# The last normalization of a sorted expert layer: computed on VectorE or on GpSimd

## The chip, the cores and the metric

The kernel runs on one core of a Trainium2 chip as a single program. The metric is the device time of one execution in microseconds (us), lower is better. A core has five engines with a queue of instructions each, which run side by side and are ordered only by semaphores: TensorE (PE in the profile: matmuls, PEld: its weight loads), VectorE (DVE), ScalarE (ACT), GpSimd (POOL) and SyncE (SP, which starts DMAs here). Each queue runs in its written order, so an instruction that waits holds everything behind it on its engine.

## The reference, cut to what matters

The reference has four sub-layers on 4096 tokens of 128 channels: a softmax attention, an attention with a mixture of experts behind it, a state-space layer, and a mixture of eight experts of which the last one selected computes a token. Each is followed by a layer norm. The change touches the very end, the layer norm behind the last mixture:

```python
def _layernorm(x, axis=-1, eps=1e-05):
    m = jnp.mean(x, axis=axis, keepdims=True)
    v = jnp.var(x, axis=axis, keepdims=True)
    return (x - m) / jnp.sqrt(v + eps)
...
    for i in range(E):
        wi = w_flat[:, i:i + 1]
        h = jax.nn.relu(jnp.einsum('nd,hd->nh', x_flat * wi, w1[i]) + b1[i])
        y = jnp.einsum('nh,dh->nd', h, w2[i]) + b2[i]
        out = jnp.where(wi > 0, y, out)
...
x = _layernorm(x + _L1_ffn_ref(x, ...), axis=-1)
```

## The kernel before, in words

Stage by stage the kernel runs the four sub-layers, with a barrier between stages. The last stage, `sorted_experts_stage` (from L1985), is the one that is changed. Before it the tokens have been sorted by expert into 40 tiles (`SORT_TILES`) of 128 tokens each, in DRAM; a record holds a token's 128 channels, its gate and the row of the output to which it belongs. The stage then works tile by tile, and every engine has a part:

- SP loads the records in 10 chunks of four tiles (`PER` is 4).
- DVE multiplies a chunk by its gates (`weigh`, L2146), PE transposes it (`turn`, L2055), ACT copies it to SBUF (`copy`, L2100).
- DVE copies the expert's first weights, 516 numbers a partition, into a ring of three (`fetch`, L2138).
- PE runs four matmuls up (L2067), ACT applies bias and ReLU to three of the four results (L2123), DVE to the fourth (`activate`, L2156), and PE runs four matmuls down (L2080), which form the tile's result in one of two places in PSUM.
- POOL adds the second bias to the residual (`add_bias`, L2217) into a ring of four (`RING` is 4).
- DVE adds that to the matmul's result (`add`, L2166), which frees the place in PSUM: `down(t)` waits for the sum of tile t-2.
- DVE takes the statistics (L2171, L2177), ACT turns the variance into 1/sqrt(variance + eps) by Ln and Exp (`invert`, L2104 and L2109), and DVE normalizes (`normalize`, L2183): one instruction, 128x128, that subtracts the mean and multiplies by the inverse, both of them one number a partition.
- POOL starts an indirect DMA that scatters the tile's 128 rows to their places in the output (`scatter`, L2222).

The order on each engine is written out by hand. DVE's loop for tile t is activate(t), fetch(t+2), statistics(t-1), for one t in four a weigh, aggregate(t-1), add(t), normalize(t-2). POOL's is add_bias(t+3), scatter(t). Rings tie them together: `add(t)` and `aggregate(t)` wait for the normalization of tile t-4, `add_bias(t)` for the sum of tile t-4, and `normalize(t)` for the landing of the scatter of tile t-4. POOL reads the tile's expert number into a register ahead of each add_bias (L2212).

Of the kernel before, what the change touches and what calls it, by code (L numbers as in the profile page):

```python
# [9 lines left out]
ALU = mybir.AluOpType  # L10
# [1779 lines left out]
SORT_TILES = (N + E * (TILE - 1)) // TILE + 1  # L1790
# [194 lines left out]
def sorted_experts_stage(core, scratch, tile_expert, w1, w2, b2, ident, out):  # L1985
# [7 lines left out]
    nc = core.nc  # L1993
# [4 lines left out]
    RING = 4  # L1998
    SLOTS = 3
    with ExitStack() as st:  # L2000
# [7 lines left out]
        total = core.sb("f_total", [TILE, RING, D], F32, st)  # L2008
        stats = core.sb("f_stats", [TILE, RING, 6], F32, st)
        mean_var = core.sb("f_mean_var", [TILE, RING, 2], F32, st)  # L2010
        log_var = core.sb("f_log_var", [TILE, RING], F32, st)
        inverse = core.sb("f_inverse", [TILE, RING], F32, st)
        normed = core.sb("f_normed", [TILE, RING, D], F32, st)
# [23 lines left out]
        with nc.Block() as block:  # L2037
# [93 lines left out]
            @block.vector  # L2131
            def _(dve):
                def fetch(t):
                    e = dve.value_load(tile_expert[0:1, t:t + 1], min_val=0, max_val=E - 1)  # L2134
                    if t >= SLOTS:
                        dve.wait_ge(low_done, t - SLOTS + 1)
                        dve.wait_ge(high_done, t - SLOTS + 1)
                    nc.vector.tensor_scalar(weights[:, t % SLOTS, :], w1[:, ds(e, 1), :].rearrange("p a n -> p (a n)"), 1.0,  # L2138
                                            None, ALU.mult).then_inc(fetched, 1)

                def weigh(c):
                    dve.wait_ge(loaded[c], 16)
                    if c >= 2:
                        dve.wait_ge(turned_done, c - 1)
                    of = slice(c * PER, (c + 1) * PER)
                    nc.vector.tensor_tensor(weighted[:, c % 2, :, :], records[:, of, 0:D],  # L2146
                                            records[:, of, D:D + 1].broadcast_to([TILE, PER, D]),
                                            ALU.mult).then_inc(weighted_done, 1)

                def activate(t):  # L2150
                    dve.wait_ge(up_done, t + 1)
                    if t >= 2:
                        dve.wait_ge(down_done, t - 1)
                    for f in range(BY_ACT, HIDDEN):
                        at = f - BY_ACT
                        last = nc.vector.tensor_scalar(high[:, t % 2, at, :], high_ps[:, t % 2, at * TILE:(at + 1) * TILE],  # L2156
                                                       weights[:, t % SLOTS, HIDDEN * D + f:HIDDEN * D + f + 1],
                                                       0.0, ALU.add, ALU.max)
                    last.then_inc(high_done, 1)

                def add(t):
                    dve.wait_ge(biased_done, t + 1)
                    if t >= RING:
                        dve.wait_ge(normed_done, t - RING + 1)
                    dve.wait_ge(down_done, t + 1)
                    nc.vector.tensor_tensor(total[:, t % RING, :], out_ps[:, t % 2, 0:D], biased[:, t % RING, :],  # L2166
                                            ALU.add).then_inc(total_done, 1)

                def spread_of(t):
                    dve.wait_ge(total_done, t + 1)  # L2170
                    nc.vector.bn_stats(stats[:, t % RING, :], total[:, t % RING, :]).then_inc(stats_done, 1)  # L2171

                def aggregate(t):
                    dve.wait_ge(stats_done, t + 1)
                    if t >= RING:
                        dve.wait_ge(normed_done, t - RING + 1)
                    nc.vector.bn_aggr(mean_var[:, t % RING, :], stats[:, t % RING, :]).then_inc(mean_var_done, 1)  # L2177

                def normalize(t):
                    dve.wait_ge(inverse_done, t + 1)  # L2180
                    if t >= RING:
                        dve.wait_ge(scattered[t % RING], 16 * (t // RING))
                    nc.vector.tensor_scalar(normed[:, t % RING, :], total[:, t % RING, :], mean_var[:, t % RING, 0:1],  # L2183
                                            inverse[:, t % RING:t % RING + 1], ALU.subtract, ALU.mult).then_inc(normed_done, 1)

                nc.vector.memset(eps[:, :], EPS).then_inc(eps_set, 1)
                fetch(0)
                fetch(1)
                weigh(0)
                weigh(1)  # L2190
                for t in range(SORT_TILES):
                    activate(t)
                    if t + 2 < SORT_TILES:
                        fetch(t + 2)
                    if t:
                        spread_of(t - 1)
                    if t % PER == 1 and t // PER + 2 < CHUNKS:
                        weigh(t // PER + 2)
                    if t:
                        aggregate(t - 1)  # L2200
                    add(t)
                    if t >= 2:
                        normalize(t - 2)
                spread_of(SORT_TILES - 1)
                normalize(SORT_TILES - 2)
                aggregate(SORT_TILES - 1)
                normalize(SORT_TILES - 1)

            @block.gpsimd
            def _(pool):  # L2210
                def add_bias(t):
                    e = pool.value_load(tile_expert[0:1, t:t + 1], min_val=0, max_val=E - 1)  # L2212
                    if t % PER == 0:
                        pool.wait_ge(loaded[t // PER], 16)
                    if t >= RING:
                        pool.wait_ge(total_done, t - RING + 1)
                    nc.gpsimd.tensor_tensor(biased[:, t % RING, :], records[:, t, 0:D],  # L2217
                                            b2[:, ds(e, 1), :].rearrange("p a n -> p (a n)"), ALU.add).then_inc(biased_done, 1)

                def scatter(t):  # L2220
                    pool.wait_ge(normed_done, t + 1)
                    nc.gpsimd.indirect_dma_start(out, bass.IndirectOffsetOnAxis(ap=records[:, t, D + 1:D + 2].bitcast(U32), axis=0),  # L2222
                                                 normed[:, t % RING, :], None).then_inc(scattered[t % RING], 16)

                for t in range(RING - 1):
                    add_bias(t)
                for t in range(SORT_TILES):
                    if t + RING - 1 < SORT_TILES:
                        add_bias(t + RING - 1)
                    scatter(t)  # L2230
                for r in range(RING):
                    pool.wait_ge(scattered[r], 16 * (SORT_TILES // RING))

# [208 lines left out]
```

## Time and profile before

| | us |
|---|---|
| median of three runs | 1810.93 (1808.12 to 1813.86) |
| the profiled execution | 1810.93 |
| its span, from the first to the last instruction | 1808.9 |
| the last stage, from SP's first load of records (1704.12) to the end of the span | 104.8 |

The profiled execution is 2.0 us longer than its span. Its granted TensorE clock is 0.921 of full speed on average over the span. Busy time is the time in which an engine runs an instruction; register, branch, semaphore and DMA-issuing instructions are not counted, but the indirect DMA on POOL is, for the time in which POOL prepares it. An arrow in a row (`<-DVE f_normed L2183`) names what ended the idle time ahead of the instruction. Tiles of the last stage have names that begin with f_.

### The profile page before, as it was taken

How to read it: one execution, taken by the hardware profiler on the slowest of the kernel's cores; microseconds unless marked ns; L12 is line 12 of the kernel's file. 1: busy time of each engine (PE TensorE's matmuls, PEld its weight loads, DVE VectorE, ACT ScalarE, POOL GpSimd, SP SyncE). 2: the span in 40 equal slices, each digit the busy share in tenths (PEclk: the TensorE clock that was granted, in tenths of full speed). 3: DMA queues.
4: the chain of work that ended last, by engine and by line, in shares of the span. 5: the costliest groups of instructions: out<-in, count | busy, mean ns of one | idle time of the engine just before them, and what ended most of it. 6: DMA issues, size and time to landing. Idle time of an engine off the chain costs nothing. (4 is left out here: it accounts for less than half of the span.)

```text
span 1808.9 us, 38945 instructions
## 1 busy us (share of the span) xinstructions
PE 1559.3 (86%) x13976; PEld 841.8 (47%) x13976; DVE 1310.8 (72%) x1816; ACT 1262.9 (70%) x2366; POOL 525.5 (29%) x742
## 2 busy tenths in 40 slices
PE   5999999999979999999999999949999653662297
PEld 4555555555534444434344443337777221222286
DVE  3777777777679999999999999334554459655176
ACT  2777777777637998898899998838887577131165
POOL 0222222222144101100100111029999033213566
PEclk8999999999978999999999999879999866785599
DMA  2021110000013110010011000034554000022300
GB/s 79 22 87 52 52 22 18 17 18 17 17 31 110 27 26 4 13 31 10 5 31 33 16 25 4 1 49 96 85 84 67 15 0 0 0 111 77 96 30 32
DMA packets 40102, 68.39 MB, mean 38 GB/s; under 512 B 9192, under 2 KB 20208, under 8 KB 39472
## 3 DMA queue, kind: packets, MB, share of 16 engines
q1 hardware_dynamic: 34608, 59.87, 14.1%
q0 software_dynamic: 5376, 6.96, 1.4%
q8 instruction: 72, 1.18, 0.3%
q14 instruction: 46, 0.38, 0.1%
HBM read 32.56 MB, written 7.77 MB: 22 GB/s over the span
## 5 line engine op out<-in xcount | busy, mean ns | idle before, releaser
L903 ACT ACTIVATE m_probs<-m_ring 128x512 f32<-128x512 f32 x1024 | 543.3, 598 | 83.4 <-PE m_ring L825 67.5
L972 DVE TENSOR_REDUCE m_half_max<-m_pairs 128x2 f32<-128x1024 f32 x512 | 587.7, 1212 | 12.6 <-PE m_pairs L808 12.1
L387 DVE TENSOR_REDUCE a_neg_max<-a_scores 128x1 f32<-128x1024 f32 x257 | 310.4, 1214 | 91.0 <-PE a_scores L314 91.0
L375 ACT ACTIVATE a_probs<-a_scores,a_neg_max 128x1024 f32<-128x1024 f32 x256 | 285.1, 1114 | 123.5 <-DVE a_neg_max L387 123.5
L840 PE MATMUL m_acc<-m_probs,m_v_aug 128*32 128x256 f32 (+1 forms) x4032 | 330.6, 401 | 0.0
L825 PE MATMUL m_ring<-m_q_max,m_k 32*128 32x512 f32 x1024 | 319.6, 503 | 3.8 <-DVE m_q_max L986 2.9
L808 PE MATMUL m_pairs<-m_k,m_q 32*128 32x512 f32 x1024 | 264.0, 513 | 13.1 <-DVE m_half_max L972 9.6
L314 PE MATMUL a_scores<-a_q,a_k_own 64*128 64x512 f32 x516 | 260.1, 620 | 6.5 <-ACT a_probs L375 5.6
L314 PE MATMUL a_scores<-a_q,a_k_other 64*128 64x512 f32 x516 | 258.4, 620 | 0.7 <-ACT a_probs L375 0.2
L825 PEld LDWEIGHTS m_ring<-m_q_max,m_k 32*128 32x128 f32 x1024 | 146.7, 184 | 219.2 <-ACT m_probs L903 115.0
L422 POOL TENSOR_TENSOR a_scaled<-values,a_inv 128x128 f32<-128x128 f32 x256 | 102.1, 399 | 389.0 <-DVE a_inv L405 258.0
L1403 POOL TENSOR_TENSOR e_g_parts<-e_gated,e_g_parts 128x512 fp32r<-128x512 f32 x128 | 165.1, 1319 | 32.9 <-ACT e_g_parts L1343 31.9
L1374 DVE TENSOR_TENSOR e_gated<-e_up,e_gates 128x512 f32<-128x512 f32 x128 | 87.5, 689 | 97.2 <-ACT e_up L1336 82.6
L324 PE MATMUL a_mixed<-a_probs,a_scaled 128*32 128x128 f32 x4128 | 139.3, 276 | 0.0
L840 PEld LDWEIGHTS m_acc<-m_probs,m_v_aug 128*32 128x32 f32 x4032 | 80.4, 109 | 125.4 <-ACT m_probs L903 79.0
L324 PEld LDWEIGHTS a_mixed<-a_probs,a_scaled 128*32 128x32 f32 x4128 | 104.9, 109 | 56.2 <-issue 30.3
L314 PEld LDWEIGHTS a_scores<-a_q,a_k_other 64*128 64x128 f32 x516 | 86.0, 187 | 65.3 <-issue 32.8
L808 PEld LDWEIGHTS m_pairs<-m_k,m_q 32*128 32x128 f32 x1024 | 97.5, 187 | 28.1 <-DVE m_half_max L972 23.2
L1336 ACT ACTIVATE e_up<-e_up,e_b 128x512 f32<-128x512 f32 x128 | 84.4, 659 | 33.7 <-PE e_up L1298 33.5
L314 PEld LDWEIGHTS a_scores<-a_q,a_k_own 64*128 64x128 f32 x516 | 86.0, 187 | 33.3 <-issue 24.4
L1054 POOL CAST m_max_cols<-m_row_max 128x16 fp32r<-128x16 f32 x32 | 6.8, 211 | 281.3 <-DVE m_row_max L978 280.8
L1309 PE MATMUL e_acc<-e_g_parts,m_q 128*128 128x512 f32 x256 | 80.2, 395 | 2.9 <-POOL e_g_parts L1403 2.9
(256 smaller groups left out, 2086.6 us busy)
## 6 DMA issues: line engine op xcount, KB each, us to landing
e_gates<-sorted_results SPq DMA_DIRECT2D x64, 256.0 KB, 8.0
a_k_other<-a_k_own SPq DMA_DIRECT2D x66, 128.0 KB
m_k<-m_k_init SPq DMA_DIRECT2D x8, 512.0 KB, 3.9
m_q<-xT SPq DMA_DIRECT2D x8, 512.0 KB, 4.4
sorted_tokens<-q_blank SPq DMA_DIRECT2D x5, 544.0 KB, 6.4
f_records<-sorted_tokens SPq DMA_DIRECT2D x10, 272.0 KB, 5.2
e_w<-e_w_dram SPq DMA_DIRECT2D x1, 2064.0 KB, 7.8
xT<-x_t_dram SPq DMA_DIRECT2D x1, 2048.0 KB, 7.7
```

Of the source, the lines that this page charges most:

```text
L314: last = nc.tensor.matmul(scores[:, slot(i), h * BANK:(h + 1) * BANK], keys[rows, p, g // 2, :], q[rows, p, :, :].rearrange("p g t -> p (g ...
L324: last = nc.tensor.matmul(mixed[32 * j:32 * j + 32, :], scaled[:, g, j, 32 * e:32 * e + 32], probs[:, g, (2 * j + e) * TILE:(2 * j + e + 1 ...
L375: nc.scalar.activation(probs[:, g, :], scores[:, slot(h * G + g), :], ACT.Exp, bias=neg_max[:, g:g + 1], accum_out=total[:, g:g + 1]).then ...
L387: nc.vector.tensor_reduce(neg_max[:, i % G:i % G + 1], scores[:, slot(i), :], AX, ALU.max, negate=True).then_inc(max_done, 1)
L422: nc.gpsimd.tensor_tensor(scaled[:, g, :, :].rearrange("p j (e c) -> p j e c", c=48)[:, :, :, 0:16], values[:, ds(b * G, G), 16 * g:16 * g ...
L808: last = nc.tensor.matmul(pairs[:, pair % 2, m, :], q[batch % 2][rows, g, at:at + TILE], k[batch % 2][rows, g, a * BANK:(a + 1) * BANK], s ...
L825: nc.tensor.matmul(o, k[batch % 2][rows, n % GROUPS, u * TILE:(u + 1) * TILE], q_max[rows, number % 2, :], start=True, stop=True).then_inc ...
L840: last = nc.tensor.matmul(acc[32 * j:32 * j + 32, of], v_aug[:, g, u, j, :], probs[:, u % SLOTS, j, of], start=(g == 0 and u == 0), stop=( ...
L903: nc.scalar.activation(probs[:, u % SLOTS, head, :], ring[:, bank, :], ACT.Exp, scale=0.5).then_inc(ring_taken, 1)
L972: nc.vector.tensor_reduce(half_max[:, pair // PAIRS % 2, at:at + 2], pairs[:, pair % 2, :, :], AX, ALU.max).then_inc(pair_taken, 1)
L1374: nc.vector.tensor_tensor(gated[:, n % R, :], up[:, n % R, :], gates[:, c % 2, e, :], ALU.mult).then_inc(gated_done, 1)
L1403: nc.gpsimd.tensor_tensor(g_parts[:, 1, n % R, :], gated[:, n % R, :], g_parts[:, 0, n % R, :].bitcast(F32), ALU.subtract).then_inc(lo_don ...
```

## The change

The instruction that normalizes a tile moves from DVE to POOL, just ahead of the scatter that reads it, and POOL waits for its own result before it issues the scatter. POOL prepares the biased residual two tiles ahead of the scatter's tile instead of three. The two loops:

```diff
@@ DVE
-                def normalize(t):
-                    dve.wait_ge(inverse_done, t + 1)
-                    if t >= RING:
-                        dve.wait_ge(scattered[t % RING], 16 * (t // RING))
-                    nc.vector.tensor_scalar(normed[:, t % RING, :], total[:, t % RING, :], mean_var[:, t % RING, 0:1],
-                                            inverse[:, t % RING:t % RING + 1], ALU.subtract, ALU.mult).then_inc(normed_done, 1)
...
                     add(t)
-                    if t >= 2:
-                        normalize(t - 2)
                 spread_of(SORT_TILES - 1)
-                normalize(SORT_TILES - 2)
                 aggregate(SORT_TILES - 1)
-                normalize(SORT_TILES - 1)
@@ POOL
-                def scatter(t):
+                def normalize(t):
+                    pool.wait_ge(inverse_done, t + 1)
+                    if t >= RING:
+                        pool.wait_ge(scattered[t % RING], 16 * (t // RING))
+                    nc.gpsimd.tensor_scalar(normed[:, t % RING, :], total[:, t % RING, :], mean_var[:, t % RING, 0:1],
+                                            inverse[:, t % RING:t % RING + 1], ALU.subtract, ALU.mult).then_inc(normed_done, 1)
                     pool.wait_ge(normed_done, t + 1)
                     nc.gpsimd.indirect_dma_start(out, bass.IndirectOffsetOnAxis(ap=records[:, t, D + 1:D + 2].bitcast(U32), axis=0),
                                                  normed[:, t % RING, :], None).then_inc(scattered[t % RING], 16)
-                for t in range(RING - 1):
-                    add_bias(t)
+                add_bias(0)
+                add_bias(1)
                 for t in range(SORT_TILES):
-                    if t + RING - 1 < SORT_TILES:
-                        add_bias(t + RING - 1)
-                    scatter(t)
+                    if t + 2 < SORT_TILES:
+                        add_bias(t + 2)
+                    normalize(t)
```

POOL's queue in the middle of the stage, two tiles of before. Square brackets hold the semaphores that an instruction waits for; TENSOR_LOAD and ISA are the reading of the expert's number and its address:

```order
L2217 TENSOR_TENSOR f_biased<-f_records,e_b 128x128
L2222 DMA out_dram<-f_normed,f_records 9216x128 [waits f_normed_done]
L2212 TENSOR_LOAD tile_expert
L2212 ISA x2
L2217 ISA [waits f_total_done]
L2217 TENSOR_TENSOR f_biased<-f_records,e_b 128x128
L2222 DMA out_dram<-f_normed,f_records 9216x128 [waits f_normed_done]
```

The same place on POOL after the change (the lines of the file have moved by 6 to 11):

```order
L2206 TENSOR_TENSOR f_biased<-f_records,e_b 128x128
L2213 TENSOR_SCALAR f_normed<-f_total,f_mean_var,f_inverse 128x128 [waits f_scattered3,f_inverse_done]
L2216 DMA out_dram<-f_normed,f_records 9216x128 [waits f_normed_done]
L2201 TENSOR_LOAD tile_expert
L2201 ISA x2
L2206 ISA [waits f_total_done]
L2206 TENSOR_TENSOR f_biased<-f_records,e_b 128x128
L2213 TENSOR_SCALAR f_normed<-f_total,f_mean_var,f_inverse 128x128 [waits f_scattered0,f_inverse_done]
L2216 DMA out_dram<-f_normed,f_records 9216x128 [waits f_normed_done]
```

Each pair of bias and scatter has become a row of three, and the scatter's wait is now for the instruction right ahead of it.

DVE's queue in the middle of the stage, one tile of before:

```order
L2171 BN_STATS f_stats<-f_total 128x6 [waits f_total_done]
L2177 BN_AGGR f_mean_var<-f_stats 128x2 [waits f_normed_done,f_stats_done]
L2166 TENSOR_TENSOR f_total<-f_out_ps,f_biased 128x128 [waits f_down_done,f_normed_done,f_biased_done]
L2183 TENSOR_SCALAR f_normed<-f_total,f_mean_var,f_inverse 128x128 [waits f_scattered2,f_inverse_done]
L2156 TENSOR_SCALAR f_high<-f_high_ps,f_weights 128x128 [waits f_down_done,f_up_done]
```

And the same place on DVE after the change:

```order
L2171 BN_STATS f_stats<-f_total 128x6 [waits f_total_done]
L2177 BN_AGGR f_mean_var<-f_stats 128x2 [waits f_normed_done,f_stats_done]
L2166 TENSOR_TENSOR f_total<-f_out_ps,f_biased 128x128 [waits f_down_done,f_normed_done,f_biased_done]
L2156 TENSOR_SCALAR f_high<-f_high_ps,f_weights 128x128 [waits f_down_done,f_up_done]
```

The normalization is gone from between the sum and the next tile's activation, and the waits for f_normed_done, which stay, are now waits for POOL. The queues of PE, ACT and SP are the same.

## Rows read from the trace of the kernel before

**Rows 1.** The page's busy times of each engine, whole span.
```profile
PE 1559.3 (86%) x13976; PEld 841.8 (47%) x13976; DVE 1310.8 (72%) x1816; ACT 1262.9 (70%) x2366; POOL 525.5 (29%) x742
```

**Rows 2.** Busy times in two stretches: columns stretch, length, engines, PEclk, DMA share, GB/s.
```profile
1752.56:1761.44 8.88, 8.04 (x68) 7.75 (x68) 6.78 (x27) 6.00 (x21) 6.41 (x9) 1.00 0.10 33
1780.07:1797.76 17.69, 17.38 (x145) 16.58 (x143) 13.11 (x51) 12.53 (x45) 12.87 (x18) 1.00 0.09 31
```

**Rows 3.** Timeline of POOL: start, length, instruction, idle before it, releaser.
```profile
1753.30 1.18 POOL L2222 DMA_INDIRECT out_dram<-f_normed,f_records  x1 [0.49 <-DVE f_normed L2183]
...
1755.96 0.98 POOL L2222 DMA_INDIRECT out_dram<-f_normed,f_records  x1 [0.99 <-DVE f_normed L2183]
1756.97 0.46 POOL L2217 TENSOR_TENSOR f_biased<-f_records,e_b 128x128 f32<-128x128 f32 x1
1757.81 0.98 POOL L2222 DMA_INDIRECT out_dram<-f_normed,f_records  x1 [0.37 <-DVE f_normed L2183]
1758.82 0.46 POOL L2217 TENSOR_TENSOR f_biased<-f_records,e_b 128x128 f32<-128x128 f32 x1
1759.77 0.98 POOL L2222 DMA_INDIRECT out_dram<-f_normed,f_records  x1 [0.48 <-DVE f_normed L2183]
1760.78 0.91 POOL L2217 TENSOR_TENSOR f_biased<-f_records,e_b 128x128 f32<-128x128 f32 x1
```

**Rows 4.** Timeline of DVE, the same stretch.
```profile
1757.16 0.37 DVE L2183 TENSOR_SCALAR f_normed<-f_total,f_mean_var,f_inverse 128x128 f32<-128x128 f32 x1
...
1760.64 0.74 DVE L2146 TENSOR_TENSOR f_weighted<-f_records 128x512 f32<-128x512 f32 x1
```

**Rows 5.** Timeline of PE, at the start of a group of four tiles.
```profile
1761.44 0.66 PE L2055 MATMUL f_turned<-consts_sb,f_weighted 128*128 128x128 f32 x4 [0.85 <-DVE f_weighted L2146]
```

**Rows 6.** Lines grouped, 1700 to 1810 us: count, busy, mean ns, idle before.
```profile
L2222 POOL DMA_INDIRECT out_dram<-f_normed,f_records x40 | 40.4, 1011 | 33.0 <-DVE f_normed L2183 32.7 <-issue 0.3
...
L2217 POOL TENSOR_TENSOR f_biased<-f_records,e_b 128x128 f32<-128x128 f32 x40 | 22.0, 553 | 8.6 <-DMA f_records<-sorted_tokens 7.5
...
L2183 DVE TENSOR_SCALAR f_normed<-f_total,f_mean_var,f_inverse 128x128 f32<-128x128 f32 x40 | 13.7, 342 | 0.9 <-ACT f_inverse L2109 0.6 <-issue 0.2
```

**Rows 7.** Lines grouped by shape, POOL, whole span.
```profile
L1054 POOL CAST m_max_cols<-m_row_max 128x16 fp32r<-128x16 f32 x32 | 6.8, 211 | 281.3 <-DVE m_row_max L978 280.8
...
L1036 POOL COPY m_v_aug<-values 128x128 f32<-128x128 f32 x16 | 4.5, 291 | 113.0 <-PE m_acc L840 113.0
```

**Rows 8.** Timeline of POOL where two elementwise instructions follow each other.
```profile
571.02 0.61 POOL L1046 CAST m_high<-m_plain 128x512 fp32r<-128x512 f32 x1 [8.64 <-ACT m_plain L908]
571.71 1.28 POOL L1048 TENSOR_TENSOR m_low<-m_plain,m_high 128x512 fp32r<-128x512 f32 x1
```

**Rows 9.** Timeline of all engines, first inverse, first normalization, first scatter.
```profile
1717.25 0.20 ACT L2109 ACTIVATE f_inverse<-f_log_var 128x1 f32<-128x1 f32 x1
...
1719.62 0.34 DVE L2183 TENSOR_SCALAR f_normed<-f_total,f_mean_var,f_inverse 128x128 f32<-128x128 f32 x1
...
1720.23 0.98 POOL L2222 DMA_INDIRECT out_dram<-f_normed,f_records  x1 [10.51 <-DVE f_normed L2183]
```

**Rows 10.** Timeline of all engines, the last matmuls and the last two scatters.
```profile
1798.84 0.48 PE L2080 MATMUL f_out_ps<-e_w,f_high 128*128 x2
...
1801.59 0.96 POOL L2222 DMA_INDIRECT out_dram<-f_normed,f_records  x1 [0.30 <-DVE f_normed L2183]
1802.85 0.96 POOL L2222 DMA_INDIRECT out_dram<-f_normed,f_records  x1 [0.30 <-issue]
```

**Rows 11.** Busy times in two earlier stretches, columns as in rows 2.
```profile
1560.00:1580.00 20.00, 15.56 (x29) 6.31 (x29) 10.86 (x9) 1.19 (x2) 4.47 (x2) 0.83 0.00 0
1600.00:1620.00 20.00, 15.10 (x32) 5.50 (x32) 9.81 (x16) 9.57 (x16) 0.56 (x1) 1.00 0.62 251
```

## The prediction, written before the changed kernel was run

> **What bounds the kernel now.** I read the page's busy times first. POOL looks idle: 29% of the span, the least of the five [rows 1]. That is an average over stages, and the change lies in one stage of 105 us at the very end, so the next view is the busy time of stretches inside it. A steady group of four tiles takes 8.88 us, in which PE is busy 8.04, DVE 6.78, ACT 6.00 and POOL 6.41. In the last stretch, where no chunk is left to be weighed, 17.69 us hold 17.38 us of PE and 12.87 of POOL [rows 2]. TensorE's granted clock is 1.00 in both, its level of 2.4 GHz.
>
> Then the timelines. PE has one real gap in a group: 0.85 us ahead of the transposes, which ends with DVE's weigh [rows 5], and DVE reaches the weigh late because its written order puts sums, activations, fetches and normalizations ahead of it. So PE and DVE share the bound in the groups. POOL is the one to look at closely. Its pattern per tile is a scatter of 0.98 us, 0.03 us of nothing, a biased residual of 0.46 us, and a pause of 0.37 to 0.99 us that each time ends with DVE's normalization [rows 3]. The shortest pause is no slack: DVE's normalization begins at 1757.16 and lasts 0.37 [rows 4], and the scatter starts at 1757.81, 0.28 us behind its end. That 0.28 us is what a scatter needs behind the result it waits for. (A scatter behind a scatter, with its data long there, starts after 1802.85 − 1802.55 = 0.30 us [rows 10].) So POOL's least period before the change is 0.98 + 0.03 + 0.46 + 0.28 = 1.75 us, plus what collisions add, beside the tile's 8.88/4 = 2.22 us in groups. In the last stretch the scatters' rhythm in rows 3 (1757.81 to 1759.77, 1.96 us) is near what PE gives with no turn: 8.04 us a group less 0.66 us of transposes [rows 5] is 1.85 us a tile. POOL's room is 0.1 to 0.4 us a tile.
>
> **The change, part by part.** DVE loses 40 normalizations of 0.342 us [rows 6], 13.7 us busy. Removing them helps only where DVE is late, and at most until PE alone is the bound: 8.88 − 8.04 = 0.84 us in each of seven groups, 5.9 us. This is to be had only if POOL can follow.
>
> POOL gains 40 normalizations of N us, each with a small gap ahead. Where POOL runs two elementwise instructions in a row the gap is 571.71 − 571.63 = 0.08 us [rows 8]. The scatter now waits for POOL's own result; I take 0.28 us again, as behind DVE's. The read of the expert number runs in POOL's sequencer while the scatter is being prepared and stays hidden, as now. The move from three tiles ahead to two delays nothing by itself: a residual is prepared at the same place of POOL's row, ahead of tile t's scatter before and ahead of the next tile's normalization now.
>
> N has no row: POOL runs no tensor-scalar in this kernel. Nearest rows: a copy of 128x128 f32 with one input takes 0.291 us, a cast of 16 elements 0.211 [rows 7]; the tensor-tensor of the same 128x128 with two inputs takes 0.46 [rows 3]. The new one has one full input and two single numbers a partition, so it lies from 0.29 up. From above, a cast of 512 elements (0.61 us [rows 8]) is a generous end for 128 elements with two operations. I take 0.40, between copy and two-input sum and nearer the latter, because two scalars have to be read as well.
>
> The Trainium skill, "GPSIMD Engine Reference", section 3.1, says that a one-input body of up to two operations goes at 1.03 cycles an element and a two-input one at about 2.6. The copy's row agrees with the first. By it N would be 0.29, which is my first rival below.
>
> Collisions: the biased residual averages 0.553 us over the stage beside 0.46 in a quiet place, the scatter 1.011 beside 0.98 [rows 6, 3]: 37 × 0.093 + 40 × 0.031 = 4.7 us already now. The row that shows it is the residual of 0.91 us at 1760.78, which overlaps DVE's weigh at 1760.64 to 1761.38 [rows 3, 4]. The normalization can meet the weigh and DVE's fetch too; I add 1.3 us for that and take C = 6 us.
>
> Now the sum. POOL's row from the first normalization on is 40 × (0.08 + N + 0.28 + 0.98) for normalization and scatter, and 37 × (0.03 + 0.46) for the residuals of tiles 3 to 39: 53.6 + 40N + 18.1 = 71.7 + 40N. The pause of 0.08 us is counted for all 40; the last two need none, within rounding. It can begin earlier than now. The first inverse is there at 1717.45, but DVE normalizes only at 1719.62, behind the sum of tile 2, and the first scatter starts at 1720.23 [rows 9]. With the move, POOL starts at about 1717.5, so its scatters are 2 us ahead at first. Last scatter prepared: 1717.5 + 71.7 + 40N + C = 1789.2 + 40N + C. With N = 0.40 and C = 6 this is 1811.2, beside 1802.85 + 0.96 = 1803.81 now [rows 10]: 7.4 us later. From there to the end the landing is the same 5.1 us, and the execution is 2.0 us longer than its span of 1808.9. The profiled execution, 1810.93, is also the median of the runs. **Forecast: 1810.93 + 7.4 = 1818.3, I say 1818 us.**
>
> A second way to the same: per tile POOL adds 0.08 + N = 0.48 us. A group has room of 8.88 − (6.41 + 4 × 0.03 + 4 × 0.28) = 1.23 us and must take 1.92: 0.69 us longer, seven times, 4.8 us. In the last stretch of ten tiles the least period is 2.23 us where it is about 1.9: 3.3 us. Together 8.1, less up to 2 us of head start: 6 to 8 us.
>
> What is queued behind the new wait: POOL's residual for tile t+3 stands behind tile t's scatter; DVE's sum of t+3 waits for it, and PE's down of t+5 for that sum. So a late POOL reaches PE some five tiles later, in a stage of 40.
>
> **The rivals.**
> *Cheap normalization, no change.* N = 0.29, C = 4.7: 1789.2 + 11.6 + 4.7 = 1805.5, 1.7 us later: 1812.6. For it speaks the copy's row; against it that two scalars are read. It decides where 40N + C comes under 20.0 us (5.4 us later than now), with C = 6 at N below 0.35.
> *Collisions or a dear instruction, much slower.* If every tile's normalization meets DVE's fetch of 0.43 us and loses half of it, 40 × 0.2 = 8 us come on top, with N = 0.46: 1789.2 + 18.4 + 4.7 + 8 = 1820.3, 16.5 us later: 1827. N = 0.61 with C = 6 gives 1819.6, about the same: 1827. For it speaks the residual of 0.91 us; against it that the residual meets a fetch in most tiles now and still takes 0.46. The Trainium skill, "SBUF — State Buffer", section "Who interferes with whom", says that a DVE instruction in a two-port mode, or with two SBUF inputs against a GpSimd instruction that reads SBUF, blocks the other for its whole length. Rows 3 and 4 agree for the two-input weigh; by this rule the fetch would do it too, and the sum would be this rival's.
> *Faster, because DVE is relieved.* The gap of 0.85 us ahead of the transposes goes and the groups shrink to PE's 8.04: 5.9 us, 1805. This needs POOL to run a group in 8.04, so four times 1.75 + 0.08 + N, with no collision at all, in 8.04: N = 0.18, less than POOL's cast of 16 elements. Even N = 0.29 with C = 0 ends POOL at 1800.8, 3.0 us earlier: 1808. I hold it nearly excluded.
> *The clock.* PE's busy share falls from 8.04/8.88 to about 0.85. Earlier stretches with PE busy 15.56 of 20 us had a mean granted clock of 0.83, between the levels of 1.2 and 2.4 GHz, others with 15.10 of 20 had 1.00 [rows 11]. At 0.83 a group of PE work would take 8.04/0.83 = 9.7 us, near POOL's 4 × 2.23 + 0.6 = 9.5; it would add 1 to 3 us. It belongs to the range.
>
> **How the numbers follow.** Forecast case (POOL becomes the bound, N from 0.35 to 0.5): 0.57. Cheap: 0.25. Much slower: 0.14. Faster: 0.04. Of the forecast case a tenth (0.06) falls within 0.3% of 1810.93 (5.4 us, about what a measurement of this kernel can tell from no change), and 0.01 of the cheap one below it: slower 0.51 + 0.14 = 0.65, same 0.24 + 0.06 = 0.30, faster 0.04 + 0.01 = 0.05. The range reaches over the cheap case to 1809 and over the dear one to 1830.
>
> **What would show it.** Right: in the changed profile POOL is busy nearly without pause from 1718 us on, about 1.9 us of 2.3 a tile; its idle time ahead of a scatter is 0.28 us and names POOL itself; DVE's sum waits for the residual on POOL, not for PE; the scatters come every 2.2 to 2.4 us in the last stretch; the last one ends near 1811. Wrong: the normalization at 0.30 us or less, the transposes no longer waiting for DVE and POOL still pausing for the inverse (cheap or faster case); residual or normalization at 0.8 us in most tiles, or a granted clock under 1.00 in this stage (the other side). If PE's and DVE's rows ahead of 1704 differ, the difference is not from the change.

## The result: slower by 1.1%, and the profile after

| | before | after |
|---|---|---|
| median of four runs each, us | 1812.39 (1808.12 to 1822.23) | 1834.70 (1832.00 to 1836.98) |
| ratio after to before | | 1.0114, 95% interval 1.007 to 1.0158 |
| profiled execution, us | 1810.93 | 1836.16 |
| its span, us | 1808.9 | 1834.2 |
| start of the last stage (SP's first load of records), us | 1704.12 | 1705.48 |
| end of the last scatter on POOL, us | 1803.81 | 1829.10 |
| last stage, from that start to that end, us | 99.7 | 123.6 |

The change makes the kernel slower, as forecast, but by three times as much, and the time lies outside the range given. The stage is 23.9 us longer; the other 1.4 us of the two profiled executions lie ahead of it, in code that did not change. That start wanders from 1695.6 to 1705.5 us over the kernels below, which all have the same code there. So below, the stage's length from the trace is the measure, and the ratio stands beside it. Each length is that of one profiled execution; how far it wanders from one execution of a kernel to the next was not measured.

The page of the kernel after, its span and busy times, answers to [rows 1]:

```profile
span 1834.2 us, 38947 instructions
...
PE 1569.0 (86%) x13976; PEld 844.3 (46%) x13976; DVE 1303.5 (71%) x1776; ACT 1263.5 (69%) x2366; POOL 564.7 (31%) x782
```

POOL's 31% looks as harmless as the 29% before. In 55 us in the middle of the last stage it does not. Stretch, length, busy time (and count) of PE, PEld, DVE, ACT and POOL, granted clock, DMA share, GB/s; after:

```profile
1730.00:1785.00 55.00, 44.44 (x333) 39.16 (x332) 29.48 (x104) 29.43 (x102) 48.76 (x60) 1.00 0.08 25
```

And before:

```profile
1730.00:1785.00 55.00, 49.88 (x421) 48.00 (x422) 42.18 (x155) 36.78 (x129) 39.02 (x51) 1.00 0.10 32
```

PE, DVE and ACT all do less in the same time; POOL does more. TensorE's granted clock is 1.00 in both, its level of 2.4 GHz, although PE is busy only 44.4 of 55 us after the change. POOL's timeline after, which answers to [rows 3]:

```profile
1752.82 0.80 POOL L2213 TENSOR_SCALAR f_normed<-f_total,f_mean_var,f_inverse 128x128 f32<-128x128 f32 x1
1753.90 1.26 POOL L2216 DMA_INDIRECT out_dram<-f_normed,f_records  x1 [0.28 <-POOL f_normed L2213]
1755.19 0.46 POOL L2206 TENSOR_TENSOR f_biased<-f_records,e_b 128x128 f32<-128x128 f32 x1
1755.63 0.80 POOL L2213 TENSOR_SCALAR f_normed<-f_total,f_mean_var,f_inverse 128x128 f32<-128x128 f32 x1
1756.70 1.27 POOL L2216 DMA_INDIRECT out_dram<-f_normed,f_records  x1 [0.28 <-POOL f_normed L2213]
```

There is no pause left but the 0.28 us of the scatter's wait for POOL's own result. One tile takes 2.80 us (1753.90 to 1756.70), and DVE waits for POOL, in DVE's timeline of the same stretch:

```profile
1752.88 0.29 DVE L2166 TENSOR_TENSOR f_total<-f_out_ps,f_biased 128x128 f32<-128x128 f32 x1 [1.06 <-POOL f_biased L2206]
...
1753.79 0.43 DVE L2138 TENSOR_SCALAR f_weights<-e_w 128x516 f32 x1 [0.36 <-ACT f_low L2123]
...
1755.68 0.29 DVE L2166 TENSOR_TENSOR f_total<-f_out_ps,f_biased 128x128 f32<-128x128 f32 x1 [1.04 <-POOL f_biased L2206]
```

The sum at 1755.68 starts when the residual of 1755.19 is done: the wait has gone over from PE to POOL. The lines of the stage after, count, busy and mean ns, idle time before, which answer to [rows 6]:

```profile
L2216 POOL DMA_INDIRECT out_dram<-f_normed,f_records x40 | 49.0, 1225 | 11.1 <-POOL f_normed L2213 11.1
...
L2213 POOL TENSOR_SCALAR f_normed<-f_total,f_mean_var,f_inverse 128x128 f32<-128x128 f32 x40 | 32.4, 810 | 8.3 <-ACT f_inverse L2109 8.2
...
L2206 POOL TENSOR_TENSOR f_biased<-f_records,e_b 128x128 f32<-128x128 f32 x40 | 19.3, 482 | 8.8 <-DMA f_records<-sorted_tokens 7.4
...
L2166 DVE TENSOR_TENSOR f_total<-f_out_ps,f_biased 128x128 f32<-128x128 f32 x40 | 11.6, 291 | 36.8 <-POOL f_biased L2206 34.1 <-PE f_out_ps L2080 2.7
```

The normalization takes 0.810 us on POOL where DVE took 0.342, and the scatter's preparation has grown from 1.011 to 1.225 us.

### The profile page after: what moved, and what is told of

Its sections match the earlier page's. It is cut to its first block and busy times, and to the rows that moved or that the text cites. A ratio compares the mean times of both kernels' runs of the same rounds, so it can differ in the third digit from the quotient of the medians.

```text
span 1834.2 us, 38947 instructions
## 1 busy us (share of the span) xinstructions
PE 1569.0 (86%) x13976; PEld 844.3 (46%) x13976; DVE 1303.5 (71%) x1776; ACT 1263.5 (69%) x2366; POOL 564.7 (31%) x782
## 3 DMA queue, kind: packets, MB, share of 16 engines
q8 instruction: 72, 1.18, 0.3%
## 5 line engine op out<-in xcount | busy, mean ns | idle before, releaser
L1298 PE MATMUL e_up<-e_x_parts,m_q 128*128 128x512 f32 x256 | 82.3, 403 | 1.5 <-PEq L1143 1.5
```

## The experiments

**The order alone.** POOL prepares the residual two tiles ahead, the normalization stays on VectorE:

```diff
-                for t in range(RING - 1):
-                    add_bias(t)
+                add_bias(0)
+                add_bias(1)
                 for t in range(SORT_TILES):
-                    if t + RING - 1 < SORT_TILES:
-                        add_bias(t + RING - 1)
+                    if t + 2 < SORT_TILES:
+                        add_bias(t + 2)
                     scatter(t)
```

> Only the order part of the change: POOL prepares the biased residual two tiles ahead instead of three, the normalization stays on VectorE. Theory (the added instruction on POOL is the whole loss): no change, 1811 us within 0.3%, last scatter near 1804, scatter 0.98 us, residual 0.46 to 0.9 us. Rival (two tiles of lead are too few): part of the 25 us is here, VectorE's sums wait for the residual on POOL, 1815 us or more.

Measured: ratio 1.0065 (1.0038 to 1.0092), stage 108.8 us, 9.1 longer than before. The rival won. The timeline of both engines over one tile of this kernel:

```profile
1752.52 0.46 POOL L2217 TENSOR_TENSOR f_biased<-f_records,e_b 128x128 f32<-128x128 f32 x1
...
1753.02 0.29 DVE L2166 TENSOR_TENSOR f_total<-f_out_ps,f_biased 128x128 f32<-128x128 f32 x1 [0.47 <-POOL f_biased L2217]
...
1753.22 0.34 DVE L2183 TENSOR_SCALAR f_normed<-f_total,f_mean_var,f_inverse 128x128 f32<-128x128 f32 x1
...
1753.84 0.98 POOL L2222 DMA_INDIRECT out_dram<-f_normed,f_records  x1 [0.86 <-DVE f_normed L2183]
...
1754.86 0.78 POOL L2217 TENSOR_TENSOR f_biased<-f_records,e_b 128x128 f32<-128x128 f32 x1
```

The residual ends at 1752.98, DVE's sum follows at 1753.02, DVE's normalization (of the tile two behind) at 1753.22 because it stands behind the sum, the scatter 0.28 us behind that, and the next residual behind the scatter. These five form a ring, in which each waits for the one before it: 1754.86 − 1752.52 = 2.34 us a tile, with no engine full. One tile more of lead had kept the ring open; the run with two ahead and the normalization first, below, tests this.

**A copy in place of the tensor-scalar.** The last layer norm's subtraction and multiplication are left out:

```diff
-                    nc.gpsimd.tensor_scalar(normed[...], total[...], mean_var[...], inverse[...], ALU.subtract, ALU.mult).then_inc(normed_done, 1)
+                    nc.gpsimd.tensor_copy(normed[:, t % RING, :], total[:, t % RING, :]).then_inc(normed_done, 1)
```

> The changed kernel with POOL's tensor-scalar replaced by a plain copy of the same 128x128 (leaves out subtraction and multiplication of the last layer norm). Theory A (the tensor-scalar is dear by itself, 0.80 us where a copy is 0.29): POOL's period falls from 2.81 to about 2.1 to 2.3 us, some 0.5 us x 40 = 20 us come back, 1812 to 1818 us. Theory B (VectorE holds the SBUF ports when POOL's instruction wants them, and 0.4 us of the 0.80 are waiting): the copy takes 0.6 to 0.7 us in the same place, and only 5 us come back, about 1830 us.

Measured: ratio 0.9998 (0.9968 to 1.0028), stage 97.7 us, 2.0 shorter than before. POOL's timeline:

```profile
1755.56 0.43 POOL L2213 COPY f_normed<-f_total 128x128 f32<-128x128 f32 x1
1756.27 0.99 POOL L2215 DMA_INDIRECT out_dram<-f_normed,f_records  x1 [0.28 <-POOL f_normed L2213]
1757.29 0.46 POOL L2206 TENSOR_TENSOR f_biased<-f_records,e_b 128x128 f32<-128x128 f32 x1
1757.85 0.29 POOL L2213 COPY f_normed<-f_total 128x128 f32<-128x128 f32 x1
```

The copy takes 0.29 us, in some tiles 0.43 (0.332 on average), the scatter 1.00. Theory A: the place on POOL is not dear, the instruction is. The stage is 25.9 us shorter than after, where theory A expected 20, because the scatter gets shorter as well, from 1.225 to 0.997 us. This is also my first rival's case, N = 0.29, and it came out 3.7 us below the 1.7 us of loss that I had worked out for it. POOL's row, from the first copy (1712.44) to the end of the last scatter (1796.53), is 84.1 us long, and the rival's sum had 71.7 + 11.6 + 4.7 = 88.0: its gaps and collisions were too many by these 3.9 us.

**The fetch behind the statistics.** In DVE's loop of the changed kernel:

```diff
-                    if t + 2 < SORT_TILES:
-                        fetch(t + 2)
                     if t:
                         spread_of(t - 1)
...
                     if t:
                         aggregate(t - 1)
+                    if t + 2 < SORT_TILES:
+                        fetch(t + 2)
                     add(t)
```

> The changed kernel with VectorE's fetch of the weights moved behind the statistics and ahead of the sum. In the changed kernel the fetch begins 0.1 us ahead of the scatter's start in every tile and the scatter takes 1.27 us; in the tiles at the end, where no fetch is left, 1.05 to 1.07. Theory (the scatter is held while a fetch runs that began before it): scatter back to about 1.06 us, period 2.6 us, 34 x 0.21 = 7 us less, 1828 us. Rival (the longer scatter belongs to running behind a tensor-scalar, not to the fetch): scatter stays at 1.27, 1835 us. Should the fetch now meet the residual or the normalization instead, those grow by up to 0.4 us and nothing is won.

Measured: ratio 1.0117 (1.0056 to 1.0177), stage 119.2 us, 4.4 shorter than after. POOL's timeline, with the scatter of a tile in which DVE weighs a chunk at 1752.49 and the next one at 1755.32:

```profile
1752.49 1.24 POOL L2216 DMA_INDIRECT out_dram<-f_normed,f_records  x1 [0.28 <-POOL f_normed L2213]
...
1755.32 1.07 POOL L2216 DMA_INDIRECT out_dram<-f_normed,f_records  x1 [0.28 <-POOL f_normed L2213]
```

And DVE's fetch in this stage, busy, mean ns, idle before:

```profile
L2138 DVE TENSOR_SCALAR f_weights<-e_w 128x516 f32 x39 | 25.5, 654 | 21.6 <-issue 18.8 <-ACT f_low L2123 2.8
```

Three of four scatters are back at 1.07 us. So it was the fetch that lengthened them: in the kernel after it starts at 1753.79, 0.11 us ahead of the scatter at 1753.90, and the scatter takes 1.26. The fourth, at 1752.49, takes 1.24 again: it starts while DVE weighs a chunk (1752.12 to 1752.80). The fetches, which now begin in the middle of a scatter, take 0.654 us instead of 0.436. The gain of 4.4 us is less than the 7 expected: the scatters give 40 × (1.225 − 1.088) = 5.5 us, since one in four keeps a collision, and the residuals, which now start beside the rest of a fetch, take 40 × (0.522 − 0.482) = 1.6 us of it back. The ratio, 1.0117 beside 1.0114 after, does not show the gain; it rests on the two traces.

The Trainium skill, "SBUF — State Buffer", section "Who interferes with whom", says that whichever of the two starts first holds the shared ports for its whole instruction. The traces agree only in part. A scatter that starts 0.11 us behind a fetch loses 0.2 us, while 0.32 us of the fetch are still to run, and a fetch that starts 0.1 us behind a scatter loses nothing (the kernel with one scalar, below).

**The instruction measured by itself.** Behind the last scatter of the kernel before, rows of four POOL instructions of a form each, then more beside 24 fetches on VectorE:

```diff
+                probe(lambda k: nc.gpsimd.tensor_scalar(normed[:, k, :], total[:, k, :], m(k), v(k), ALU.subtract, ALU.mult))
+                probe(lambda k: nc.gpsimd.tensor_scalar(normed[:, k, :], total[:, k, :], v(k), None, ALU.mult))
+                probe(lambda k: nc.gpsimd.tensor_scalar(normed[:, k, :], total[:, k, :], 0.5, 2.0, ALU.subtract, ALU.mult))
...
```

> The kernel before, and behind its last scatter a row of POOL instructions four times each: tensor-scalar 128x128 with two scalars a partition, with one, with two constants, with one constant, copy, the first form on 16 and on 64 elements, the first form in turn with a tensor-tensor, all with VectorE idle, and then the first form and the tensor-tensor while VectorE repeats its fetch. Their results are thrown away (the normalized tiles are already written out). The time is longer by the probe, some 40 us, and only the lengths count. Theory A (dear by itself): 0.80 us with VectorE idle for two scalars, less with fewer scalars or constants. Theory B (ports): about 0.4 us with VectorE idle, 0.8 beside the fetches. Theory C (the cost is POOL changing from one kind of instruction to another): 0.3 to 0.5 us in a row of its own kind, 0.8 in turn with the tensor-tensor.

Measured, the lines of POOL behind the last scatter, count, busy, mean ns, idle before:

```profile
L2268 POOL TENSOR_SCALAR f_normed<-f_total,f_mean_var,f_inverse 128x128 f32<-128x128 f32 x4 | 4.1, 1032 | 0.1
L2258 POOL TENSOR_SCALAR f_normed<-f_total,f_mean_var,f_inverse 128x128 f32<-128x128 f32 x4 | 3.1, 792 | 1.5 <-DMA out_dram<-f_normed,f_records 1.5
...
L2260 POOL TENSOR_SCALAR f_normed<-f_total 128x128 f32<-128x128 f32 x4 | 2.5, 644 | 0.1
L2259 POOL TENSOR_SCALAR f_normed<-f_total,f_inverse 128x128 f32<-128x128 f32 x4 | 2.4, 603 | 0.1
L2269 POOL TENSOR_TENSOR f_normed<-f_total,f_biased 128x128 f32<-128x128 f32 x4 | 2.3, 614 | 0.1
L2264 POOL TENSOR_SCALAR f_normed<-f_total,f_mean_var,f_inverse 128x64 f32<-128x64 f32 x4 | 2.2, 578 | 0.1
L2261 POOL TENSOR_SCALAR f_normed<-f_total 128x128 f32<-128x128 f32 x4 | 2.0, 530 | 0.1
L2263 POOL TENSOR_SCALAR f_normed<-f_total,f_mean_var,f_inverse 128x16 f32<-128x16 f32 x4 | 1.7, 429 | 0.1
L2262 POOL COPY f_normed<-f_total 128x128 f32<-128x128 f32 x4 | 1.0, 291 | 0.1
```

With DVE idle, a row of its own kind takes 0.792 us (L2258): theory A. One scalar a partition: 0.603 (L2259). Two constants: 0.644 (L2260), one constant: 0.530 (L2261). A copy: 0.291 (L2262). The full form on 64 elements takes 0.578 and on 16 it takes 0.429, so by my estimate an element costs (0.792 − 0.578)/64 = 3.3 ns and the start of an instruction about 0.37 us. Theory C falls with the first row, which is dear among its own kind. DVE's fetches ran beside L2265 to L2269, L2266 included, since POOL's signal to DVE ran ahead of POOL's own work; beside them the full form takes 1.03 us and the tensor-tensor 0.61 instead of 0.46, so a collision costs 0.15 to 0.25 us on top but does not make the 0.79. The change from one kind to the other was therefore not seen here without fetches. It can be read in the kernel after: there the tensor-scalar follows a tensor-tensor or a scatter, in 38 of 40 tiles with no fetch beside it, and takes 0.80 us, so the change costs 0.01 us at most.

**The order undone, the normalization on POOL.** The changed kernel with `RING - 1` tiles of lead again, the first diff backwards.

> The changed kernel with its order part undone: POOL prepares the residual three tiles ahead again, the normalization stays on POOL. With the normalization on VectorE the order alone cost 9 us (108.8 us for the last stage instead of 99.7), because VectorE's normalization of tile t stands behind its sum of t+2, which waits for the residual of t+2. Theory (that ring of waits doesn't exist when POOL normalizes; POOL's own row is the bound whatever its order): no change to the changed kernel, stage 123.6 us within 1, 1835 us. Rival (the order costs its 9 us here too): stage near 115 us, 1826 us.

Measured: ratio 1.0134 (1.0084 to 1.0184), stage 122.8 us against 123.6. POOL's timeline:

```profile
1755.92 0.80 POOL L2213 TENSOR_SCALAR f_normed<-f_total,f_mean_var,f_inverse 128x128 f32<-128x128 f32 x1
1757.00 1.27 POOL L2216 DMA_INDIRECT out_dram<-f_normed,f_records  x1 [0.28 <-POOL f_normed L2213]
```

The row is the same as after: 0.80, 0.28 and 1.27 us. With the normalization on POOL the sum of tile t+2 no longer stands ahead of it, and POOL's own work is the bound in either order.

**One scalar instead of two.** The subtraction of the mean is left out:

```diff
-                                            inverse[:, t % RING:t % RING + 1], ALU.subtract, ALU.mult).then_inc(normed_done, 1)
+                    nc.gpsimd.tensor_scalar(normed[:, t % RING, :], total[:, t % RING, :], inverse[:, t % RING:t % RING + 1],
+                                            None, ALU.mult).then_inc(normed_done, 1)
```

> The changed kernel with POOL's instruction cut to one multiplication by one number a partition (leaves out the subtraction of the mean). Behind the last scatter this form took 0.60 us where the full one took 0.79. Theory (POOL's row is the bound, each nanosecond of its instruction counts 40 times): stage 123.6 - 40 x 0.19 = 116 us, POOL's period 2.6 us, 1828 us. Rival (the loss is in collisions with VectorE's fetch, which fall otherwise for another length): the stage changes by some other amount, from 110 to 124 us, with scatters or instructions of other lengths.

Measured: ratio 1.0068 (1.0045 to 1.0091), stage 109.7 us, 13.9 shorter than after where 7.6 were expected. Its lines, count, busy, mean ns, idle before:

```profile
L2216 POOL DMA_INDIRECT out_dram<-f_normed,f_records x40 | 41.1, 1027 | 11.1 <-POOL f_normed L2213 11.1
...
L2213 POOL TENSOR_SCALAR f_normed<-f_total,f_inverse 128x128 f32<-128x128 f32 x40 | 25.3, 633 | 8.2 <-ACT f_inverse L2109 8.1
L2206 POOL TENSOR_TENSOR f_biased<-f_records,e_b 128x128 f32<-128x128 f32 x40 | 20.9, 525 | 8.6 <-DMA f_records<-sorted_tokens 7.4
```

The instruction gives 40 × (0.810 − 0.633) = 7.1 us, as the theory said. Another 40 × (1.225 − 1.027) = 7.9 us come from the scatters, which now start 0.1 us ahead of the fetch instead of behind it, and 37 × (0.525 − 0.482) = 1.6 us go back to residuals. Together 13.4. A scatter of this kernel:

```profile
1750.60 1.02 POOL L2216 DMA_INDIRECT out_dram<-f_normed,f_records  x1 [0.28 <-POOL f_normed L2213]
```

DVE's fetch begins at 1750.70, inside it, and takes 0.43 us as in a quiet place; neither loses time. Both accounts were partly right: POOL's row is the bound, and a shorter instruction also shifts it against DVE's.

**Two ahead, normalization first.** DVE normalizes tile t-2 ahead of its sum of tile t, in the order-only kernel:

```diff
-                    add(t)
                     if t >= 2:
                         normalize(t - 2)
+                    add(t)
```

> VectorE normalizes, POOL prepares two tiles ahead (the order-only kernel), but VectorE's normalization of tile t-2 stands ahead of its sum of tile t. Theory (the order-only kernel's 9 us come from the ring residual(t+2), sum(t+2), normalization(t), scatter(t), residual(t+3), of 0.46 + 0.04 + 0.2 + 0.34 + 0.28 + 0.98 + 0.03 = 2.33 us a tile): the ring is cut, POOL's pause of 0.86 us shrinks, stage back to 99 to 101 us, 1809 us. Rival (two tiles of lead are too few for any other reason, such as the wait for the sum of tile t-4): stage stays near 108 us, 1817 us.

Measured: ratio 1.0009 (0.9988 to 1.0031), stage 99.4 us. POOL's timeline:

```profile
1754.83 0.99 POOL L2222 DMA_INDIRECT out_dram<-f_normed,f_records  x1 [1.24 <-DVE f_normed L2183]
...
1756.69 0.98 POOL L2222 DMA_INDIRECT out_dram<-f_normed,f_records  x1 [0.37 <-DVE f_normed L2183]
...
1759.37 0.98 POOL L2222 DMA_INDIRECT out_dram<-f_normed,f_records  x1 [1.16 <-DVE f_normed L2183]
...
1761.02 0.99 POOL L2222 DMA_INDIRECT out_dram<-f_normed,f_records  x1 [0.16 <-issue]
```

The pauses are no longer 0.86 us each. Over a group of four tiles they are 1.24, 0.37, 1.16 and 0.16 us, the first three waits for DVE as before the change, 2.9 us instead of 3.4, and the 9 us are back. The ring was their cause.

**The weigh one tile earlier.** In the kernel before:

```diff
-                    if t % PER == 1 and t // PER + 2 < CHUNKS:
+                    if t % PER == 0 and t // PER + 2 < CHUNKS:
                         weigh(t // PER + 2)
```

> The kernel before with VectorE's weigh one tile earlier (in the first of four tiles instead of the second). Theory (in a group PE's only wait of 0.85 us is for the weigh, and VectorE has room for it a tile earlier): the wait ahead of the transposes goes, groups shrink from 8.88 to about 8.2 us, stage 99.7 - 7 x 0.7 = 95 us, 1806 us. Rival (VectorE as a whole is the bound in the groups, busy 6.78 us plus its pauses for the expert's number): the wait only moves to another place and the stage stays at 99 to 100 us.

Measured: ratio 0.9962 (0.9938 to 0.9985), stage 94.0 us (1699.15 to 1793.10), 5.7 shorter than before. PE's timeline at the start of a group, which answers to [rows 5]:

```profile
1752.16 0.60 PE L2055 MATMUL f_turned<-consts_sb,f_weighted 128*128 128x128 f32 x4
...
1760.33 0.60 PE L2055 MATMUL f_turned<-consts_sb,f_weighted 128*128 128x128 f32 x4
```

The transposes have no idle time ahead, where 0.85 us stood. A group takes 1760.33 − 1752.16 = 8.2 us, as the theory said. Of the kernels here that compute everything it has the shortest stage, with the last one below beside it.

**One normalization in four on POOL.** The third of each group of four goes to POOL, with a semaphore of its own; once on the kernel before, once on the early weigh:

```diff
                 def scatter(t):
-                    pool.wait_ge(normed_done, t + 1)
+                    if t % PER == 2:
+                        pool.wait_ge(inverse_done, t + 1)
...
+                        nc.gpsimd.tensor_scalar(normed[...], total[...], mean_var[...], inverse[...], ALU.subtract, ALU.mult).then_inc(normed_pool, 1)
+                    normed_wait(pool, t)
```

> The kernel before with the normalization of one tile in four on POOL (the third of each group, ahead of its scatter), the others on VectorE, residuals three tiles ahead. Theory: POOL has 1.23 us of room in a group of 8.88 us by the prediction's second sum, and one normalization of 0.80 + 0.08 us fits into it; VectorE is relieved by 0.25 us a group where its weigh is late: stage from 98 to 100 us. Rival (POOL's room is not where the normalization needs it, and the normalization on POOL delays the scatter and the next residual): stage 102 us or more.

> Both: the weigh one tile earlier, which shortened the stage to 94.0 us with groups of 8.2 us, and one normalization in four on POOL. In a group of 8.2 us POOL's least need is 7.65 us before the addition, 8.5 with it. Theory (POOL becomes the bound again): stage about 2 us longer than with the early weigh alone, 96 us. Rival (the relief of VectorE is worth more): 92 to 94 us.

Measured: on the kernel before, a single time of 1808.11 us, stage 98.9 us, as the theory expected; one tile's 0.85 us fits into POOL's room. With the early weigh: ratio 0.9977 (0.9957 to 0.9998), stage 94.4 us, 0.5 longer than with the early weigh alone; the 2 us expected were too many. POOL's timeline there:

```profile
1755.92 0.99 POOL L2235 TENSOR_SCALAR f_normed<-f_total,f_mean_var,f_inverse 128x128 f32<-128x128 f32 x1
1757.19 1.05 POOL L2238 DMA_INDIRECT out_dram<-f_normed,f_records  x1 [0.28 <-POOL f_normed L2235]
```

The normalization takes 0.99 us here (a fetch begins at 1756.34, in the middle of it), 1.03 on average, and POOL has next to no pause in the group. VectorE is not relieved either: its thirty normalizations take 0.475 us on average, 14.2 us together, where the forty of the kernel with the early weigh alone took 13.9. Nothing is gained by it.

**Early weigh, normalization first.** The last two DVE edits together.

> The early weigh, and VectorE's normalization of tile t-2 ahead of its sum of tile t. The inverse it needs is there about 2 us before VectorE comes to it, so it can fill VectorE's wait for PE's down. Theory: it fills part of that wait and POOL's scatters start earlier, stage 93 to 94 us. Rival (it delays the sum, for which PE's down two tiles on waits): stage 95 us or more.

Measured: ratio 0.9972 (0.9948 to 0.9996), stage 94.1 us, the same as with the early weigh alone within what these runs can tell. That lies between theory and rival and shows neither a gain nor a loss.

## Why the prediction was wrong, step by step

- **POOL becomes the bound: right.** Its row has no pause from 1718.81 to the end, the pause ahead of each scatter is 0.28 us and names POOL itself, and DVE's sum waits for the residual, 34.1 us in the stage. The head start was right too: POOL's first normalization starts at 1718.81, which is 1717.45 without the 1.36 us by which this stage starts later, where 1717.5 was said. Here are both ends of POOL's row:

```profile
1718.81 0.97 POOL L2213 TENSOR_SCALAR f_normed<-f_total,f_mean_var,f_inverse 128x128 f32<-128x128 f32 x1 [8.20 <-ACT f_inverse L2109]
...
1828.05 1.05 POOL L2216 DMA_INDIRECT out_dram<-f_normed,f_records  x1 [0.28 <-POOL f_normed L2213]
```

- **N = 0.40 us: wrong, and the term that failed.** It is 0.81 us in the kernel and 0.79 by itself. That is 40 × 0.41 = 16.4 us more, nearly the whole miss. The bound from above, a cast of 512 elements at 0.61 us, was a length of another instruction and no bound. Nothing in the trace of before held the price of a tensor-scalar on POOL, and the range should have been open on that side. DVE's 0.342 us for the same instruction said nothing either.
- **The rule on one-input bodies.** The Trainium skill, "GPSIMD Engine Reference", section 3.1, gives 1.03 cycles an element for one input and up to two operations. It fits the copies and casts, which go from 0.291 us at 128 elements to 0.609 at 512, so 0.83 ns an element; by the 1.2 GHz with which that section reckons, 1.03 cycles are an estimated 0.86 ns. It does not fit the tensor-scalar, which takes 3.3 ns an element with two scalars; even with one constant the instruction takes 0.530 us.
- **Collisions, C = 6 us: low, and for the wrong instruction.** The scatter takes 1.225 us on average, not 0.98: 9.8 us. About a third of that is no collision, for behind a tensor-scalar it takes 1.05 to 1.07 us even with no fetch beside it; the rest are 32 scatters with 0.2 us more, each 0.1 us behind the start of a fetch. The residual takes 0.482 instead of 0.46: 0.8 us. The gap of 0.08 us ahead of the normalization is not there (the next instruction is shown from 0.02 us before the end of the one ahead): 39 × 0.10 = 3.9 us less. Together 16.4 + 9.8 + 0.8 − 3.9 − 6.0 = 17.1 us over the sum; the trace shows (1829.10 − 1718.81) − 93.7 = 16.6. The terms beside N come to 0.7 us net, which is luck: collisions 4.6 us too low and gaps 3.9 us too high cancel.
- **"The residual meets a fetch in most tiles now and still takes 0.46": a wrong reading,** on which the low chance of the dear rival rested. In the trace of before the residual meets a fetch in 2 of 40 tiles, and the scatter meets one in 35. Two fetches beside the scatters of 1753.30 and 1757.81 in [rows 3]:

```profile
1753.20 0.41 DVE L2138 TENSOR_SCALAR f_weights<-e_w 128x516 f32 x1
...
1758.00 0.43 DVE L2138 TENSOR_SCALAR f_weights<-e_w 128x516 f32 x1 [0.21 <-DVE f_high L2156]
```

The first began 0.10 us ahead of its scatter, which took 1.18 us; the second began 0.19 us behind its scatter, which took 0.98. Six scatters of before had such a fetch just ahead and took 1.17 or 1.18. So the price of this collision stood in the trace, hidden in the mean of 1.011; the change made six such tiles into 32.

- **"The move from three tiles ahead to two delays nothing by itself": wrong as written.** By itself it costs 9.1 us. In this change it costs nothing, as said, because the normalization leaves DVE. I had looked at the place of the residual in POOL's row, but not at what POOL's scatter waits for on DVE.
- **The second way to the same sum** agreed with the first because it took the same N. Two sums from one unmeasured number are one sum.
- **The cheap rival** (N = 0.29) was tried: no change, as it said. **The faster one** needed N = 0.18; the copy shows that with 0.29 the stage is 2.0 us shorter. **The dear one** came nearest, 1827 us. Its first form had a meeting with the fetch, but on the wrong instruction: the scatter pays, not the normalization. Its second form, a dear instruction, had the larger cause, and its N = 0.61 was still 0.2 us short. **The clock** played no part: from 1715 us to the last matmuls the granted clock is 1.00 after as before. It is lower only in the stage's first 10 us, 0.51 in both, and at the very end, when PE has no work left (0.51 from 1824 to 1829 us after, 0.84 from 1800 to 1803.8 before).

## What to carry to other kernels

Before work is moved to an engine that looks idle, its period in the stage concerned is to be added up, and the instruction timed there in its exact form: two instructions of the same size on the same engine differed here by 2.7 times. Where such a price is missing, the range has to be open upward. Which instruction meets which is to be read from the start times of both, and a mean that is a little long is to be split into its cases: 1.011 us hid scatters of 0.98 and of 1.18. A change of how far ahead one engine works is checked by following the whole ring of waits through the other engines' written orders; here the same edit cost 9.1 us or nothing, depending on one instruction's place. And the wait that did bound the kernel was cured by moving the late instruction itself, for 5.7 us.

## What the runs showed of the hardware

- POOL's tensor-scalar on 128x128 f32: 0.79 us with two scalars a partition, 0.60 with one, 0.64 with two constants, 0.53 with one constant, against 0.29 for a copy and 0.46 for a tensor-tensor in a quiet place.
- The indirect DMA's preparation depends on what ran ahead of it on POOL: 0.96 us behind another one, 0.98 behind the tensor-tensor, 1.00 behind a copy, 1.05 to 1.07 behind the tensor-scalar, each without a fetch beside it. Why is open.
- It takes 0.2 us more when DVE's fetch of 516 elements has begun 0.1 us ahead of it (1.18 instead of 0.98 before, 1.27 instead of 1.06 after). When the fetch begins 0.1 to 0.3 us behind it, neither loses time (0.98 and 0.43 in most tiles of before). When the fetch begins 0.6 us behind it, the fetch takes 0.71 us (later fetch). Beside a train of such fetches POOL's tensor-scalar goes from 0.79 to 1.03 us, and the median fetch from 0.43 to 0.56.
- A scatter whose data are long there starts 0.16 or 0.17 us behind a residual, and 0.28 us behind the result it waits for. POOL's least period before the change is so 0.1 us shorter than the prediction had it. In the kernel with the early weigh:

```profile
1752.93 0.46 POOL L2217 TENSOR_TENSOR f_biased<-f_records,e_b 128x128 f32<-128x128 f32 x1
1753.56 0.99 POOL L2222 DMA_INDIRECT out_dram<-f_normed,f_records  x1 [0.17 <-issue]
```
